# Gated attention and expert block: the first attention step written out by hand, loads on two queues, contexts loaded as 112 and 13 rows

## The reference

```
x = x + tanh(g_xattn) * cross_attention(layernorm(x), ctx)     # x (32, 56, 128), ctx (32, 1500, 128)
#   q = ln(x) Wq' + bq, k = ctx Wk' + bk, v = ctx Wv' + bv; softmax(q k' / sqrt(8)) v per head; then Wo, bo
x = x + tanh(g_ffn) * experts(layernorm(x))
#   probs = sigmoid(x router' + bias); the 8 largest, normalised, times 2.5, weigh
#   silu(x w_gate[e]') w_down[e]' of each of 160 experts (64 wide); one shared expert besides
```

## Time and profile before

| | |
|---|---|
| median of 3 runs | 1201.7 us |
| lowest, highest | 1195.89, 1203.61 us |
| the profiled execution | 1199.14 us |
| its span | 1197.6 us |
| mean granted TensorE clock | 0.979 |
| busy: PE, DVE, ACT, POOL | 1099.4, 979.5, 837.8, 599.5 us |
| PE's share of the span | 92% |

### The profile page before, as it was taken

One profiled execution on the slowest core, in us unless ns is written; L12 is line 12 of the kernel. 1 busy time (PEld: TensorE's weight loads), 2 busy tenths in 40 slices (PEclk: granted clock), 3 DMA queues, 4 the chain that ended last, 5 costly groups with the idle time before them and its releaser, 6 DMA issues.

```text
span 1197.6 us, 37798 instructions
## 1 busy us (share of the span) xinstructions
PE 1099.4 (92%) x12090; PEld 704.8 (59%) x12090; DVE 979.5 (82%) x1680; ACT 837.8 (70%) x1790; POOL 599.5 (50%) x1011
## 2 busy tenths in 40 slices
PE   1586989999999999999999999877999999999998
PEld 0254667767766667767766676653555555555554
DVE  2774768878788788787887888757999999999998
ACT  1343656676666676676667666656888888888887
POOL 7887588888888887888888772000000000000000
PEclk9887999999999999999999999988999999999999
DMA  8869668969878789798887863123777676777773
GB/s 134 156 124 162 140 134 174 151 149 166 145 163 154 139 169 146 152 164 145 168 151 139 168 118 74 41 90 108 225 234 234 223 240 222 236 230 229 237 224 125
DMA packets 200998, 197.04 MB, mean 165 GB/s; under 512 B 161183, under 2 KB 167391, under 8 KB 200966
## 3 DMA queue, kind: packets, MB, share of 16 engines
q1 hardware_dynamic: 189446, 175.64, 65.4%
q0 software_dynamic: 11520, 20.99, 7.0%
HBM read 109.96 MB, written 12.55 MB: 102 GB/s over the span
## 4 chain that ended last, share of the span: by engine, by line
PE 75%; DVE 7%; ACT 5%; issue 4%; DMA 4%; SPq 3%; POOL 2%; ACTq 0%; DVEq 0%; POOLq 0%
PE bank L1230 14%; PE bank L1258 14%; PE bank L1069 12%; PE bank L1083 12%; PE bank L1100 8%; PE bank L1136 5%; ACT p_exp L640 4%; PE bank L1124 4%; DMA ctT<-ctx_parts 3%; DVE rec L938 2%; DVE part_max L838 1%; SPq L378 1%; PE bank L1155 1%; DVE ctT L980 1%; PE bank L1148 1%
## 5 line engine op out<-in xcount | busy, mean ns | idle before, releaser
L640 ACT ACTIVATE p_exp<-bank 125x448 f32<-125x448 f32 x768 | 389.6, 546 | 241.9 <-PE bank L1083 241.3
L838 DVE TENSOR_REDUCE part_max<-bank 128x1 f32<-128x500 f32 x672 | 419.5, 671 | 111.5 <-PE bank L1100 110.9
L1083 PE MATMUL bank<-q_st,k_stk 97*125 97x224 f16 x1536 | 282.9, 268 | 23.7 <-ACT p_exp L640 6.9
L1100 PE MATMUL bank<-kparts,q_blk 128*128 128x500 f16 x672 | 256.3, 384 | 17.8 <-DVE part_max L838 13.2
L1083 PEld LDWEIGHTS bank<-q_st,k_stk 97*125 97x125 f16 x1536 | 184.2, 138 | 130.4 <-ACT p_exp L640 75.9
L1258 PE MATMUL bank<-ctT,w_ring 128*128 128x448 f16 x960 | 234.0, 353 | 3.0 <-DVE ctT L980 3.0
L732 ACT ACTIVATE ctT<-bank 128x448 f32<-128x448 f32 x320 | 174.0, 544 | 40.0 <-PE bank L1230 15.8
L980 DVE TENSOR_TENSOR ctT<-k_stk,ctT 128x448 f16<-128x448 f32 x320 | 198.0, 619 | 0.3 <-ACT ctT L738 0.2
L1069 PE MATMUL bank<-p_exp,v_sb 125*25 125x168 f32 (+1 forms) x6144 | 189.2, 264 | 0.6 <-ACT p_exp L640 0.6
L738 ACT ACTIVATE ctT<-k_stk 128x448 f16<-128x448 f32 x320 | 181.9, 568 | 3.5 <-DVE k_stk L974 3.5
L1230 PE MATMUL bank<-q_hi,w_ring 128*128 128x448 f16 x640 | 173.9, 353 | 2.2 <-ACT k_stk L720 2.2
(11 more groups left out here) (139 smaller groups left out, 1244.8 us busy)
## 6 DMA issues: line engine op xcount, KB each, us to landing
v_sb<-c_scratch SPq DMA_DIRECT2D x114, 448.0 KB, 3.9
k_stk<-kparts SPq DMA_DIRECT2D x384, 93.8 KB, 5.0
ctx_in<-in_ctx_dram SPq DMA_DIRECT2D x31, 750.0 KB
k_stk<-c_scratch SPq DMA_DIRECT2D x38, 448.0 KB, 4.0
w_scratch<-w_out POOLq DMA_DIRECT2D x80, 128.0 KB, 6.7
w_in<-in_L_ffn_w_gate_dram POOLq DMA_DIRECT2D x160, 32.0 KB, 4.5
w_in<-in_L_ffn_w_down_dram POOLq DMA_DIRECT2D x80, 64.0 KB, 7.7
v_sb<-c_scratch SPq DMA_DIRECT2D x6, 336.0 KB, 4.8
```

Of the source, the lines that this page charges most:

```text
L640: act.activation(p_exp[0:KP, j % PR, f * 448:(f + 1) * 448], ST[f][0:KP, 0:448], ACT.Exp).then_inc(exp_done, 1)
L838: v.reduce_max(part_max[:, i // NCH, i % NCH:i % NCH + 1], SM[i % NSM][:, 0:CK], axis=AX.X).then_inc(sm_maxed, 1)
L1083: last = pe.matmul(ST[f][0:KP, (g % 2) * GC:(g % 2 + 1) * GC], k_stk[0:97, u, g, j * KP:(j + 1) * KP], q_st[0:97, u, g, :, :].rearrange("p ...
L1100: pe.matmul(SM[i % NSM][:, 0:CK], rows, kparts[:, u, 0, c * CK:(c + 1) * CK], start=True, stop=True).then_inc(sm_done, 1)
```

## The change

- **SP's inputs.** SP loads the first quarter of x, context 0 in three chunks (chunk 0 now ahead of the weights) and the four attention weights. The padding rows, the biases, the other x and context 1 are issued by ACT, before all its other work.
- **112 and 13 rows.** Each context load is two DMAs, of rows 0 to 111 and of rows 112 to 124 (`load_rows`); the semaphores count 32 for one load (`CTX`).
- **Step 0 by hand.** PE, ACT and DVE start `attention` at step 1. The keys of context 0 are projected before it, each chunk into its own PSUM bank (`FKB`), with the queries of the first quarter between chunks 0 and 1.
- **Queries.** The scale 1/sqrt(8) is put into `wqT`, so DVE makes `q_lo` with one instruction instead of two. The rest of the layer norm and of the queries moves from step 0 to step 1: DVE centres before step 1, ACT squares with a sum per token group (12 small instructions) and also scales (12 more); the queries' banks are `QB`.
- **SP's order.** The copies of the first queries and `ones_rows` move behind the transposes of context 1. Of the rest of the queries two thirds are copied in step 2 and one in step 3, instead of one each in steps 1, 2 and 3. `output_rows` moves from the start of step 2 to the starts of steps 3 and 4, eight each.
- **POOL.** Constants come after the splits of context 0; the first 15 weight loads move to the start of step 2, and every expert pair is prepared two steps later. The wait for the first query rows moves behind the splits.
- **PE.** The shared weights' transposes move to (1, 9); waits for queries, ones and the cleared output bank to (2, 1) and (2, 4); the wait for output rows to its use.

```diff
+    VAR_REST_AT, RSTD_REST_AT, SCALE_REST_AT = (1, 1), (1, 2), (1, 3)
+    TOKENS_REST_AT = {(1, 5): (1, 3), (1, 8): (3, 4)}
+    SHARED_AT, GATES_AT, CONSTANT_AT, QUERIES_FREE_AT, OUT_FREE_AT = (1, 9), (1, 11), (2, 1), (2, 1), (2, 4)
...
+        FKB = [KB, SM[2], SM[1]]
...
-        REST_ROWS_AT = {1: (0,), 2: (1,), 3: (2,)}
+        REST_ROWS_AT = {2: (0, 1), 3: (2,)}
+        QB = [bank[0], bank[0], bank[1], bank[0]]
+        CTX = 32
...
+        def load_rows(eng, here, dst, src):
+            for p0, p1 in ((0, 112), (112, KP)):
+                eng.dma_start(dst[p0:p1], src[p0:p1]).then_inc(here, 16)
...
-            load_x(*FIRST, x_in)
+            load_x(sp, *FIRST, x_in)
+            load_chunk(0)
             for n, w in enumerate((Wq, Wk, Wv, Wo)):
                 sp.dma_start(w_raw[:, n, :], w).then_inc(weights_in, 16)
-            load_chunk(0)
...
-            load_x(*REST, x_rest)
-            sp.dma_start(ctx_in[0:KP, 1, :, :], ctx[1].rearrange("(p j) c -> p j c", j=KT)).then_inc(ctx_here[1], 16)
...
+            def first_queries():
+                stack_queries(0, 1, (0, 2, 1), q_rows)
+                ones_rows()
...
-            attention(sp, body, B - 2, {2: output_rows})
+            attention(sp, body, B - 2, {1: first_queries, 3: lambda: output_rows(0, H // 2),
+                                        4: lambda: output_rows(H // 2, H)})
...
+                for c in range(NCH):
+                    if on(step, -1):
+                        split_ctx(back(step, -1), c)
+                    if on(step, 2):
+                        expert_pairs(back(step, 2), PREP[step[1]][c:c + 1])
                 if isinstance(step[0], int) and num(step) == 1:
                     first_rows()
...
-            attention(pool, body, B - 2, {3: add_constant, 4: all_rows})
+            attention(pool, body, B - 2, {2: first_pairs, 3: add_constant, 4: all_rows})
...
+            def square_rest():
+                act.wait_ge(ln_sub, 2)
+                for p in range(*REST):
+                    last = act.activation(sq_rest[:, p - PPC, :], xc[:, p, :], ACT.Square, accum_out=stat[:, 0, p:p + 1])
+                last.then_inc(ln_sq, 1)
+
+            def scale_rest():
+                act.wait_ge(rstd_made, 1)
+                for p in range(*REST):
+                    last = act.activation(xc[:, p, :], xc[:, p, :], ACT.Copy, scale=stat[:, 4, p:p + 1])
+                last.then_inc(ln_done, 1)
...
+            load_x(act, *REST, x_rest)
+            load_rows(act, ctx_here[1], ctx_in[0:KP, 1, :, :], ctx[1].rearrange("(p j) c -> p j c", j=KT))
             act.wait_ge(o_cleared, 2)
...
+            first_keys(0)
             act.wait_ge(bqs_made, 1)
             queries(0, 1)
+            first_keys(1)
+            first_keys(2)
+            square_rest()
...
+            def first_keys(c):
+                pe.wait_ge(t_here[c], 16)
+                for i, (w, part) in enumerate(((wk_hi, 0), (wk_lo, 0), (wk_hi, 1))):
+                    last = pe.matmul(FKB[c][:, 0:CK], w[:, :], ctT[:, 0, c, part, :, 0:KP], start=(i == 0), stop=(i == 2))
+                last.then_inc(kp_done, 1)
```

More of the change, by code:

```diff
@@ L243, in until, with attention @@
                 eng.wait_ge(s, value)
-        def attention(eng, body, loop_to=B, before={}):
-            for s in range(4):
+        def attention(eng, body, loop_to=B, before={}, first=0):
+            for s in range(first, 4):
                 if s in before:
@@ L276, in row, with load_x @@
             return ap.rearrange("(a n) -> a n", a=1)
+        def load_rows(eng, here, dst, src):
+            for p0, p1 in ((0, 112), (112, KP)):
+                eng.dma_start(dst[p0:p1], src[p0:p1]).then_inc(here, 16)
+        def load_x(eng, p0, p1, here):
+            for b in range(2):
+                eng.dma_start(xt[b * T:(b + 1) * T, p0:p1, :],
+                              x.rearrange("(n b) t c -> b t n c", b=2)[b, :, p0:p1, :]).then_inc(here, 16)
         gate_pairs = w_gate.rearrange("(n e) i h -> n e i h", e=2)
@@ L541, in _ @@
                 split_ctx((0, 0), c)
-            for i in range(WPP):
-                load_pair(0, i)
+            const(pool.memset(den_spread[:, :], 0.0))
+            const(pool.affine_select(out=den_spread[:, :].rearrange("p (g n) -> p g n", g=4),
+                                     in_=den_spread[:, :].rearrange("p (g n) -> p g n", g=4),
+                                     compare_op=ALU.not_equal, fill=1.0,
+                                     base=3 * d, pattern=[[32, 4], [0, 32]], channel_multiplier=-1))
+            assert made[0] == MASKS
+            const(pool.memset(k_stk[96:97, 0, 0, :], 1.0))
+            assert made[0] == K_ONES
+            const(pool.memset(v_sb[:, :, :, 0:4, 3 * d:VW], 1.0))
+            const(pool.memset(v_sb[:, :, :, 4:VG, d:VW], 1.0))
+            assert made[0] == V_ONES
             pool.wait_ge(q_hi_done, 1)
@@ L577, in body, with first_pairs @@
                     last.then_inc(qst_made, 1)
-            attention(pool, body, B - 2, {3: add_constant, 4: all_rows})
+            def first_pairs():
+                for i in range(WPP):
+                    load_pair(0, i)
+            attention(pool, body, B - 2, {2: first_pairs, 3: add_constant, 4: all_rows})
         @block.scalar
@@ L612, in _ @@
                 act.wait_ge(wp_tr, n + 1)
-                act.activation(w[:, :], bank[n][:, 0:D], ACT.Copy).then_inc(wp_cp, 1)
+                act.activation(w[:, :], bank[n][:, 0:D], ACT.Copy, scale=QSCALE if n == 0 else 1.0).then_inc(wp_cp, 1)
             root(1, *FIRST)
@@ L709, in evacuate @@
                                        ACT.Identity, bias=bkc[:, 0:1]).then_inc(k_hi_done, 1)
-            attention(act, body, B, {1: gates_and_shared})
+            attention(act, body, B, first=1)
             load_root_table(4, sq_late, stat[:, 2, 0:1])
@@ L860, in body @@
                                         negate=True).then_inc(neg_made, 1)
[L861 to L862 removed]
+                    aside(step, k, (VAR_REST_AT, variance_rest), (RSTD_REST_AT, rstd_rest),
+                          *((at, lambda c=c: queries(*c)) for at, c in Q_LO_REST_AT.items()),
                           (CONSTANT_AT, constant_term),
@@ L943, in normalise @@
                                 o_raw[:, :].rearrange("p (n t) -> p n t", t=T), ALU.mult).then_inc(nrm_done, 1)
-            attention(dve, body)
+            attention(dve, body, first=1)
             dve.wait_ge(x2_done, NP)
@@ L1096, in maxima @@
                 until(pe, sm_maxed, b * (MT * NCH) + (i - (NSM - 1)))
+                if i == 0 and not on(step, 2):
+                    pe.wait_ge(k_lo_done, NCH)
                 if i == NSM - 1:
@@ L1213, in weights_out @@
                     last.then_inc(cb_tr, 1)
-            attention(pe, body, B, {1: shared_and_router})
+            attention(pe, body, B, first=1)
             hilo = ((0, 0), (1, 0), (0, 1))
```

136 lines of the change are left out of this document (63 added, 73 removed).

## The result

| | before | after |
|---|---|---|
| median | 1201.93 us of 4 runs | 1182.78 us of 4 runs |
| lowest, highest | 1195.89, 1203.61 | 1180.6, 1184.41 |
| the profiled execution | 1199.14 | 1180.6 |
| its span | 1197.6 | 1179.1 |

The ratio is 0.9849, with a 95% interval from 0.9816 to 0.9882: 1.5% faster. The forecast was 1180, its range 1170 to 1191.

The account below looks back on a forecast made before the run. SP's queue was taken to bound the first stages and PE everything after 178.7 us. 17.0 won at the first score plus 4.6 in step 2 made 21.6: 1177.5 profiled, 1180 on the median, range 1170 to 1191.

Parts of the forecast that it names:

- The window that can win: The stages before 178.7 us: only there can the change win, as PE bounds the kernel afterwards; 17.3 lost in four steps.
- SP's inputs free at about 6, ACT not held: Input loads at the start: SP free at about 6 instead of 13.0, ACT's nine issues hidden; 1 to 2 taken.
- Transposes of context 0, 7.5 to 16.5, ends 14.5 and 20.5: SP's first three transposes: paced by the splits, done at 16.5, at best 14.5, at worst 20.5; they took 12.96 before.
- Threes of contexts 1 and 2 at 8 each, ends 6 and 10.4: SP's three transposes behind a context load: 8 us per context instead of 10.37 and 9.59, between 6 and 10.4.
- What else of SP's chain: SP's other work before the first score: small inputs 4.0, query rows and ones 7.6 + 1.5, key rows 7.6.
- far ends: The late bounds of SP's transpose terms: first score at 65.7, 8.6 won there, 13.2 in all, 1188.
- Step 2 at 27.1: From the first score of step 2 to that of step 3: 27.1 instead of 31.7, 4.6 won; ends 24.8 and 31.7.
- No gain in the loop: The 24 loop steps and the end: no change, as SP waits 79.6 us for PE's values there.
- POOL the bound of the loop: Rival: new register work per expert pair makes POOL bound the loop, 1217 at 1.3 a pair; slower loop 0.07.
- Narrow all the same: Rival: 112 and 13 rows still run narrow, so 1188; gain mostly returned or late bounds of the transposes together 0.20.
- The loop gains too: Rival: half of PE's 11.5 us outside its work vanish in the loop, 6 more, 1174 or 1168; under 1173: 0.13.
- Given back at the lower clock: Rival: steps 2 to 4 cost 28 to 29 each, 8 to 10 given back, 1186 to 1192; part of a 0.20 case.

Follow-up runs that it names:

- ctx1_late: The changed kernel with context 1 issued by ACT after its small early work instead of before it; median 1180.25 us, ratio 0.9833.
- changed_again: The changed kernel run once more, unaltered; median 1181.71 us, ratio 0.9845 to the kernel before.
- wo_first: The changed kernel with all sixteen output rows back at the start of step 2; median 1187.66 us, ratio 0.9903 to the kernel before.
- rest_rows_2: The changed kernel with all three thirds of the other query rows copied in step 2; median 1179.69 us, ratio 0.9851 to the kernel before.
- one_piece: The changed kernel with each context load as one DMA of 125 rows again; median 1198.74 us, ratio 0.9986 to the kernel before.
- rows_alone: The kernel before with only its context loads split in 112 and 13 rows, all on SP; median 1192.24 us, ratio 0.9925.

## Why the prediction was right

The median came 2.8 above the forecast and inside the range. The place and the kind of the gain were as forecast; that the first score came near its number was luck, since two of its terms were wrong by 7.0 and 5.3 in opposite directions. By its steps:

- **The window that can win.** Right: 18.5 of span are 21.8 won up to step 5 and 3.3 lost behind it (1.6 of the 21.8, in step 5, come and go without an edit).
- **SP's inputs free at about 6, ACT not held.** SP's last issue ended at 7.6, 1.6 later than forecast; it cost nothing, as the first split ended at 8.06. ACT's square came at 7.12. Right.
- **Transposes of context 0, 7.5 to 16.5, ends 14.5 and 20.5.** This is the term that was mis-sized. They ended at 23.5, beyond the far end, 7.0 late. I let POOL's splits set the pace; in fact the data of chunk 1 did, behind a first transpose that alone held SP for 5.40. I had looked at when loads are issued, and not at what the 16 DMA engines move in the time: chunk 1 waits for the weights in its own queue and shares with what ACT issued (ctx1_late has it at 13.43 instead of 15.0 to 18.65). The repeat (changed_again) has the end at 21.5, still beyond the far end.
- **Threes of contexts 1 and 2 at 8 each, ends 6 and 10.4.** 4.79 and 5.87, 5.3 less in sum, both below the near end. The row nearest was not the old three behind a narrow load but the three free ones of 3.7. I had left out POOL here: I costed the expert pairs moved out of steps 0 and 1 at nothing, and with the width alone the threes stay at 8.06 and 11.14, with all but the width at 5.74 and 10.82.
- **What else of SP's chain.** Small inputs 3.8 for 4.0, query rows and ones 9.3 for 9.1, key rows 8.6 for 7.6. Between, SP stood 1.6 for POOL's first split of context 1, not in the sum. With +7.0, -5.3, +1.0, +1.6 and 0.3 of small ones the first score comes 4.6 later than 57.3: 61.9. One error covered the other. A slip of addition besides: with the far ends as stated (20.5, and twice 10.4) the first score is at 66.1, not 65.7, which moves the price of the far ends from 1188 to 1189.
- **Step 2 at 27.1.** 25.2. The third transpose ended at 79.98, 18.1 after the first score, where I took 19.7 from a row with a narrow load in front of it.
- **Output rows moved: covered.** Steps 3 and 4 are 23.5 and 25.2 (forecast 24.8 and 25.2). wo_first gives the price of not moving them, 5 in step 2.
- **Step 4 is POOL's wait for the last query rows.** Right, shown by rest_rows_2.
- **No gain in the loop.** Right in kind: SP's room grew by 94 us to no use. Not foreseen: 1.6 lost to DVE and POOL in each other's way. The tail, where I said no change, lost 1.7 in this profile, but over all fourteen profiles it lies between 495.5 and 498.8 (496.8 in the repeat), so the 1.7 may be scatter.
- **Rivals.** *POOL the bound of the loop*: refuted, its gap is 0.7 still. *Narrow all the same*: refuted by the DMA slices; but its price was too low: I gave 1188 for it and one_piece measured 1198.74, with the loads on one queue 1192.00. I had not seen that a second queue of narrow loads costs. *The loop gains too*: refuted. *Given back at the lower clock*: steps 2 to 4 took 25.2, 23.5 and 25.2, not 28 to 29. In the window 28.5 to 61.9 the granted mean is 0.76, where the two like stages before had 0.99 and 0.80; the chain there goes over SP's transposes, for which PE still waits 4.98 at 60.22, so I take it that this cost little; no run shows it.
- **The rule against the second queue** (the Trainium skill, "DMA: Bandwidth & Descriptors", section "Issuing engines are not separate DMA queues"): the runs agree. With all loads on SP the kernel is as fast (1179.77), and with narrow loads it is faster than with two queues. The forecast credited ACT's queue with issue time only, and even that bought nothing, as the data was what came late.

What stays open: whether the tail is longer at all; where the low-clock stretches in step 5 come from; why wide loads bring more products and subtractions together in the loop; and how much belongs to the hand-written step 0, to the first query rows behind the transposes of context 1 and to the moved pairs, each alone. The runs bound only all of them together: 7.1 with narrow loads and one queue (1192.00 against 1199.13), and 9.1 over rows_alone with wide ones (0.9925 less 0.9849, of 1200).

## What to carry to other kernels

Look first at how many of the DMA engines a load runs on: splitting 125 rows in 112 and 13 gave 8 us by itself. The whole reordering gave 7 us without it when all loads stood on one queue, and nothing when they stood on two; so before saying that two parts need each other, look for a third that harms one of them. Two covers over one wait (here a narrow load and the weight pairs between splits) show no gain in that wait until both are lifted. When a queue's first loads are put in a new order, add up the bytes in front of each consumer over all queues, not the issue times of one. And before moving instructions in a loop, list those whose longest time is far above their median: here a product that took 0.39 or 1.13 us was worth 5.4 us of the median, and about half of its 24 turns in the loop were long.

## What the hardware showed that I had not expected

- A DVE product of two SBUF operands that starts during a POOL subtraction ends 0.25 us after it: 1.13 instead of 0.39 us, 10 times in 24 steps (12 in the repeat). A cast or a DMA issue of POOL can do the same (0.64 to 0.77 before). With one operand in PSUM it is never longer than 0.392, in the midst of a subtraction too.
- The width of a load is paid by what is queued behind it: median issue of a transpose 2.66 with 125-row loads, 1.24 with 112 and 13; to landing 5.9 and 3.2. One transpose was held 12.99 where both queues carried narrow loads.
- A second queue for loads made nothing faster, and with narrow loads slower: first score at 76.3 with two queues, at 68.4 with one.
- Wide loads and a longer loop go together: 525.3 with them alone (rows_alone) against 522.7 before, with 11 products against 5 that end after a subtraction.
